# Causal masks of two attentions: from a matmul into the scores to an addition on VectorE

## The reference

```python
# part 1: latent self-attention, 16 heads; q and k have 128 plain and 64 rotated columns
scores = jnp.einsum('bqhd,bkhd->bhqk', q, k) * scale
causal = jnp.tril(jnp.ones((seq_len, seq_len), dtype=bool))
scores = jnp.where(causal[None, None], scores, -jnp.inf)
probs = jax.nn.softmax(scores.astype(jnp.float32), axis=-1)
out = jnp.einsum('bhqk,bkhd->bqhd', probs, v)

# part 2: cross-attention to 375 context rows, 16 heads of 32 columns
scores = jnp.einsum('bhqd,bhkd->bhqk', qh, kh) * inv_sqrt_d
causal = jnp.tril(jnp.ones((sq, sk), dtype=bool))      # row i sees context rows 0..i
scores = jnp.where(causal, scores, jnp.finfo(scores.dtype).min)
attn = jax.nn.softmax(scores, axis=-1)

# part 3: a shared feed-forward network and a mixture of 16 experts, two of them for each row
```

## Time and profile before

| | |
|---|---|
| median of three runs | 857.99 us (857.32 to 858.27) |
| the profiled execution | 858.94 us |
| its span, from first to last instruction | 857.1 us |
| TensorE busy | 827.0 us, 96% |
| VectorE busy | 518.0 us, 60% |
| ScalarE busy | 470.3 us, 55% |
| Pool busy | 241.7 us, 28% |
| granted TensorE clock, mean | 0.996 |

### The profile page before, as it was taken

One profiled execution on the slowest core, in us unless ns is written; L12 is line 12 of the kernel. 1 busy time (PEld: TensorE's weight loads), 2 busy tenths in 40 slices (PEclk: granted clock), 3 DMA queues, 4 the chain that ended last, 5 costly groups with the idle time before them and its releaser, 6 DMA issues.

```text
span 857.1 us, 13364 instructions
## 1 busy us (share of the span) xinstructions
PE 827.0 (96%) x4302; PEld 706.4 (82%) x4302; DVE 518.0 (60%) x962; ACT 470.3 (55%) x1221; POOL 241.7 (28%) x284
## 2 busy tenths in 40 slices
PE   7999999999999999999998899999999999999997
PEld 5887887888788777888877689888888988889885
DVE  4755654753664548687787566355665655646466
ACT  6427545753843556977785526063755737647050
POOL 0142320230132031655654002602233322321420
PEclk9999999999999999999999999999999999999999
DMA  9113225315132406322120113624563655644422
GB/s 336 67 44 111 74 53 152 121 43 160 73 96 51 153 23 213 87 59 57 50 70 24 53 47 85 259 85 150 174 218 117 229 172 184 199 140 144 130 79 86
DMA packets 41597, 99.99 MB, mean 117 GB/s; under 512 B 15888, under 2 KB 23952, under 8 KB 39920
## 3 DMA queue, kind: packets, MB, share of 16 engines
q1 hardware_dynamic: 30496, 61.62, 23.0%
q0 software_dynamic: 11056, 37.79, 13.6%
HBM read 71.59 MB, written 20.97 MB: 108 GB/s over the span
## 4 chain that ended last, share of the span: by engine, by line
PE 77%; issue 9%; ACT 4%; DVE 4%; SPq 2%; DMA 2%; POOL 1%; POOLq 0%; ACTq 0%; DVEq 0%
PE ps L1545 61%; PE ps L1894 2%; PE ps L1566 2%; PE ps L1778 2%; SPq L556 2%; PE ps L1605 2%; PE ps L1884 1%; ACT Pt L885 1%; PE ps L1709 1%; PE ps L1597 1%; DMA stage<-in_wa 1%; PE ps L1896 1%; PE ps L1632 1%; PE ps L1560 1%; PE ps L1718 1%
## 5 line engine op out<-in xcount | busy, mean ns | idle before, releaser
L642 POOL TENSOR_TENSOR Pt<-Pt,rowinv 112x448 f32<-112x448 f32 x64 | 59.7, 933 | 188.2 <-DVE rowinv L1155 187.8
L1545 PE MATMUL ps<-x2T_hi,ws_hi 128*128 128x448 f32 x256 | 95.8, 374 | 3.7 <-ACT h_hi L1020 3.7
L885 ACT ACTIVATE Pt<-ps,negmax 112x112 f32<-112x112 f32 x256 | 87.1, 359 | 19.3 <-DVE negmax L1148 19.1
L1545 PE MATMUL ps<-x2T_hi,ws_lo 128*128 128x448 f32 x256 | 94.3, 368 | 0.0
L1545 PE MATMUL ps<-x2T_lo,ws_hi 128*128 128x448 f32 x256 | 94.2, 368 | 0.0
L1019 ACT ACTIVATE hf<-ps,b 128x448 f32<-128x448 f32 x64 | 40.5, 633 | 93.0 <-PE ps L1545 73.9
L1545 PE MATMUL ps<-w_hi,h_hi 128*128 128x512 f32 x224 | 89.9, 401 | 0.0
L1545 PE MATMUL ps<-w_hi,h_lo 128*128 128x512 f32 x224 | 88.4, 395 | 0.0
L1545 PE MATMUL ps<-w_lo,h_hi 128*128 128x512 f32 x224 | 88.4, 395 | 0.0
L1092 DVE TENSOR_TENSOR h_lo<-hf,h_hi 128x448 fp32r<-128x448 f32 x64 | 39.8, 623 | 47.0 <-ACT h_hi L1020 46.6
L1431 DVE TENSOR_TENSOR acc<-ps,acc 128x512 f32<-128x512 f32 x56 | 38.6, 689 | 45.0 <-PE ps L1545 38.1
(11 more groups left out here) (291 smaller groups left out, 2225.8 us busy)
## 6 DMA issues: line engine op xcount, KB each, us to landing
stage<-in_wf SPq DMA_DIRECT2D x30, 513.0 KB
rows_in<-in_zeros SPq DMA_DIRECT2D x30, 256.0 KB, 4.1
xs<-rows_in POOLq DMA_DIRECT2D x29, 256.0 KB, 4.3
rows_out<-yb POOLq DMA_DIRECT2D x29, 256.0 KB
stage<-in_wa SPq DMA_DIRECT2D x4, 1408.0 KB, 6.6
stage<-in_wb SPq DMA_DIRECT2D x4, 1280.0 KB, 5.6
qr<-ro_hi SPq DMA_DIRECT2D x64, 56.0 KB, 1.9
qr<-ro_lo SPq DMA_DIRECT2D x64, 56.0 KB, 1.9
```

Source lines behind the costliest of these rows:

```text
L642: nc.gpsimd.tensor_tensor(p, p, rowinv[0:S, b % 2, :].unsqueeze(2).broadcast_to([S, GH, S]), ALU.mult).then_inc(norm_done, 1)
L885: last = nc.scalar.activation(Pt[0:S, b % 2, h * S:(h + 1) * S], ps[0:S, b % 2, h * S:(h + 1) * S], ACT.Exp, bias=negmax[0:S, b % 2, h:h + 1],
L1545: ins = mm(dst, w, x, start=start and i == 0, stop=stop and i == len(ops) - 1, skip_group_check=not (start and stop))
```

## The change

The 64 mask matmuls go, with `identb`, `maskb`, their casts and the semaphore for them. Two float32 masks stay in SBUF instead: `maskf` for scores with keys on partitions, `maskq` for scores with queries on partitions; one more transfer brings the second. In self-attention, the turned scores now leave their bank on VectorE, which adds `maskf` on the way to `sT`, at the places ("G", j) of its order; ScalarE's copy goes. In the last group VectorE's list gets a place for G7. In cross-attention, the one reduction of a batch becomes `masked_max`: a memset of a small tile, and for each head an instruction that adds `maskq` to the scores in their PSUM bank, multiplies by -1, writes the result back in place, and takes the minimum of each row, which is the negated maximum. The exponentials take the scores with a scale of -1. Pool gets one more wait, in the loop, ahead of its share of splitting the cross weights (`wx_hi`). The diff, without the places where only a count of a semaphore changes:

```diff
-    ("Z", 3), ("T", 4), ("S", 5), ("N", 5), ("Z", 4), ...
+    ("Z", 3), ("T", 4), ("S", 5), ("G", 7), ("N", 5), ("Z", 4), ...
...
-        identb = sb("identb", [P, S], BF16, at=both)
-        maskb = sb("maskb", [P, S], BF16, at=both)
+        maskf = sb("maskf", [P, S], at=both)
+        maskq = sb("maskq", [P, S], at=both)
+        touch = sb("touch", [P, 2], at=both)
...
-            for dst, name in ((ident, "ident"), (maskf, "mask"), (wnorm, "wnorm")):
+            for dst, name in ((ident, "ident"), (maskf, "mask"), (maskq, "maskq"), (wnorm, "wnorm")):
...
+                else:
+                    pool.wait_ge(x_free["V"], XJ.count(("V", 1), g - 1))
                 high(wx_hi[:, cols], stage[:, cols]).then_inc(xk_hi, 1)
...
-            copy(identb[0:S, :], ident[0:S, 0:S])
-            copy(maskb[0:S, :], maskf[0:S, :]).then_inc(const_done, 1)
...
-            def probabilities(m, b):
+            def probabilities(m, b, sign=1.0):
...
-                                                bias=negmax[0:S, b % 2, h:h + 1],
+                                                bias=negmax[0:S, b % 2, h:h + 1], scale=sign,
...
-                elif kind == "G":
-                    act.wait_ge(job_done, at.number + 1)
-                    copy(sT[0:S, j % 2, :], ps[0:S, 6 + at.bank, 0:GH * S]).then_inc(a_free["G"], 1)
...
+            def masked_max(m, b):
+
+                dve.wait_ge(sc_done, m + 1)
+                nc.vector.memset(touch[0:S, b % 2:b % 2 + 1], 0.0)
+                for h in range(GH):
+                    s = ps[0:S, b % 2, h * S:(h + 1) * S]
+                    ins = nc.vector.tensor_tensor_reduce(s, s, maskq[0:S, :], -1.0, 3.0e38, ALU.add, ALU.min,
+                                                         negmax[0:S, b % 2, h:h + 1])
+                ins.then_inc(max_done, 1)
...
+                elif kind == "G":
+                    dve.wait_ge(job_done, at.number + 1)
+                    nc.vector.tensor_tensor(sT[0:S, j % 2, :].rearrange("p (h s) -> p h s", h=GH),
+                                            ps[0:S, 6 + at.bank, 0:GH * S].rearrange("p (h s) -> p h s", h=GH),
+                                            maskf[0:S, :].unsqueeze(1).broadcast_to([S, GH, S]), ALU.add)\
+                        .then_inc(a_free["G"], 1)
...
-                    row_max(m + j, j)
+                    masked_max(m + j, j)
...
-                    mask(bank[0:S, 0:GH * S], maskb, identb)
...
-                        ins = mm(heads(bank[0:S, 0:GH * S]), w, x, start=False, stop=i == len(ops) - 1,
-                                 skip_group_check=True)
+                        ins = mm(heads(bank[0:S, 0:GH * S]), w, x, start=i == 0, stop=i == len(ops) - 1)
...
-                    mask(ps[0:S, j % 2, 0:GH * S], identb, maskb)
...
-                        ins = mm(ps[0:S, j % 2, 0:GH * S], w, x, start=False, stop=i == 2,
-                                 skip_group_check=True)
+                        ins = mm(ps[0:S, j % 2, 0:GH * S], w, x, start=i == 0, stop=i == 2)
```

More of the change, by code:

```diff
@@ L368, in build @@
         krt = sb("krt", [P, 2, HALF], at=first)
-        maskf = sb("maskf", [P, S], at=first)
         first.close()
@@ L475, in build @@
         yg_ld = [sem(f"yg_ld{i}") for i in range(4)]
-        (const_done, in_hi, in_lo, down_done, sq_done, root_done, rinv_done, nat_done,
+        (in_hi, in_lo, down_done, sq_done, root_done, rinv_done, nat_done,
          kvn_hi, kvn_lo, tr_done, tr_hi, tr_lo, kr_done, kr_mul, kr_rot, krh, krl) = map(sem, (
-            "const_done in_hi in_lo down_done sq_done root_done rinv_done nat_done kvn_hi "
+            "in_hi in_lo down_done sq_done root_done rinv_done nat_done kvn_hi "
             "kvn_lo tr_done tr_hi tr_lo kr_done kr_mul kr_rot krh krl").split())
@@ L830, in _ @@
             copy(wd_hi[:, :, D:768], wd[:, :, D:768]).then_inc(in_hi, 1)
-            act.wait_ge(c_ld, 64)
-            copy(identb[0:S, :], ident[0:S, 0:S])
-            copy(maskb[0:S, :], maskf[0:S, :]).then_inc(const_done, 1)
+            act.wait_ge(c_ld, 80)
             def squares(r):
@@ L978, in x_step @@
                 elif kind == "S":
-                    probabilities(m + j, j)
+                    probabilities(m + j, j, -1.0)
                 elif kind == "T":
@@ L1108, in _ @@
             low(wd_lo[:, :, D:768], wd[:, :, D:768], wd_hi[:, :, D:768]).then_inc(in_lo, 1)
-            dve.wait_ge(c_ld, 64)
+            dve.wait_ge(c_ld, 80)
             def rms(r):
@@ L1593, in heads @@
                 return ap.rearrange("p (h s) -> p h s", h=GH)
-            def mask(dst, w, x):
-                mm(heads(dst), w[0:S, :], x[0:S, :].unsqueeze(1).broadcast_to([S, GH, S]), start=True,
-                   stop=False, skip_group_check=True)
             def transposes(m, b):
@@ L1638, in keys_ready @@
                 pe.wait_ge(krl, 2)
-                pe.wait_ge(const_done, 1)
             def att_step(item, g, at):
@@ L1986, in layouts @@
     o["ident"] = np.eye(P, dtype=f)
-    o["mask"] = np.where(np.arange(P)[:, None] < np.arange(S), f(-3.0e38), f(0))
+    o["maskq"] = np.where(np.arange(P)[:, None] < np.arange(S), f(-3.0e38), f(0))
+    o["mask"] = np.where(np.arange(P)[:, None] > np.arange(S), f(-3.0e38), f(0))
     part = np.arange(P)
```

## The result

The changed kernel takes **870.57 us** (median; 870.25 to 872.62) against 857.65 of the kernel before on the same chip: ratio 1.0156, 95% interval 1.0138 to 1.0173. The forecast was 869, so the time came out as forecast, and slower as forecast. That the sum came out so close is in part luck: self-attention cost more than its term and cross-attention less, and two effects that were in no term, a lower clock and the place of the buffers, have opposite signs.

What follows compares the result with a forecast made beforehand. TensorE was taken to bound the kernel, but VectorE's queue to delay it in self-attention and VectorE to become the bound in cross-attention. 858.94 + 4.3 + 6.8 = 870.0, less 0.95: 869 us; range 858.5 to 880.

Steps and rivals of the forecast that it cites:

- Part 1: TensorE's mask matmuls: 64 go, 0.19 us of queue each, 12.2 us in all if nothing else moves.
- walk over the cross groups: Cross-attention loop group, order lists followed: +1.5 us at c = 1.25, 0 at 1.0, about -0.9 at 0.81.
- c: Cross-attention's masked maximum on VectorE: time from one batch's first to the next instruction, 1.25 us, +0.72 a batch.
- Part 2: Self-attention's turned scores leaving on VectorE, 32 times: late in its in-order queue, +4.3 us, bounds +3.5 to +5.5.
- the first step: Self-attention group: G1's way out stands behind SB1's low half on VectorE, so G2 starts 1.47 us later.
- The second step: End of a self-attention loop group: G5's way out comes only after N3 on VectorE, so E0 starts 1.71 us later.
- E0: TensorE's item of the next self-attention group that uses G5's bank, not a run; forecast start 162.81 instead of 161.10.
- Part 3: Cross-attention's maximum, 32 times: one reduction becomes a memset and four masked instructions on VectorE, +6.8 us.
- Part 4: Small changes: one more mask transfer, two casts gone, a new wait on Pool; 0, at worst +0.5 us.
- Slow heads: Rival, cross-attention's maximum: each instruction waits until the one before has drained, c 1.6 to 2.0, 879 to 887 us; chance 0.19.
- Cheap heads: Rival, cross-attention: c 0.8 to 1.0, TensorE keeps the bound there, 859.8 to 863.3 us; chance 0.19.
- TensorE bound everywhere: Rival, whole kernel: late places made good, c under 1, saved mask matmuls count, 846 to 855 us; chance 0.08.

Runs made afterwards that it cites:

- The part alone: Against the kernel before: under Part 2, only the self-attention change, 865.93 us, ratio 1.0087; under Part 3, only the cross-attention change, 861.31 us, ratio 1.0036.
- the wide filling: The changed kernel with 9 matmuls of no use, 448 wide, on TensorE ahead of G2 and the next group's E0: 867.94 us, ratio 1.0120.

## Why the prediction was right, and where its steps were not

- **Part 1, 0.19 us for a mask on TensorE: the price stands, the paying out did not.** The kernel without the cross mask shows 0.19 (1.00 less 0.81). The forecast never booked 12.2, but its walk over the cross groups counted 26.7 of TensorE's work as a floor that would be reached at small c. Left out, the cross masks give 1.8 us of 6.1, those of self-attention 2.5 of 6.1.
- **Part 2, the queue place: right in place, the first step right in size.** SB1's low half stands ahead (1.93 forecast, 1.92 measured); turned around, the loss goes. The second step is larger than forecast: from SB1's low half to E0 it is 17.7 in a group with the clock up between them (222.48 to 240.19), where the forecast had 17.27 and the kernel before 15.56. SA0's low half, which takes 1.27 in place of 0.96 there, is 0.3 of that; why is open. What failed is the sentence that TensorE carries the delay on unchanged: behind the longer waits it also runs at the lower clock. That step is missing from the sum; it is 3.0 to 5.4 us of the changed kernel's loss. The part alone measures +7.7 against +4.3; less its two stretches at 1.2 to 1.5 us it is +4.7 to +5.3, inside the bounds of 3.5 to 5.5. By the wide filling, which has no stretch, it is +3.9 and, without the place in SBUF, +5.7, just above them.
- **Part 3, c: mis-sized.** 0.91 instead of 1.25, because the accumulator's read runs beside the next head. ScalarE's pair of instructions was the nearest row and the wrong analogue. The 0.15 a head in the upper end had no row either; the read shows 0.14, and overlaps.
- **Part 3, what c does to the group: mis-sized the other way.** At 0.91 the walk gives about -0.7; the part alone gives +3.1, and +4.6 without the place in SBUF (5.2 in the traces). VectorE did not become the bound by its sum (24.26 of 29.60 busy, where the forecast looked for over 26); single chains lengthened: the values' low half behind two maxima, then the way out of the output. How much each of them takes is shown for the first alone. The walk, made by busy time and the share of idle time that stays, took slack for granted that no row had shown. The forecast +6.8 came near +4.6 only since the two errors have opposite signs.
- **Part 4: right**; nothing in the start of the trace after is later than before.
- **The place in SBUF, -1.4 to -1.9: not foreseen,** and not to be seen in any row of the kernel before.
- **Why 869 was hit all the same.** The clock (3.0 to 5.4 too little), the place (1.4 to 1.9 too much) and cross-attention's masked maxima (some 2 too much) were all left out or mis-sized, and they nearly cancel. That is luck; the sign and the first waits are not.
- **Rivals.** Slow heads: out, by the 0.23 a head. Cheap heads had c right (0.8 to 1.0) and the time wrong, as it rested on the same walk. TensorE bound everywhere: out twice, for self-attention by the waits, for cross-attention by the kernel without its mask, which gains only 1.8 even with no new work on VectorE.
- **The sum of the parts:** 7.7 + 3.1 = 10.8, and the changed kernel has 12.9 to 14.0; the intervals of the three are together some 2.5 us wide to each side. The number of stretches of lower clock may be the rest, as the changed kernel has more of them than the part alone in one of two traces; that is argued, not shown.

## What to carry to other kernels

Moving work from a full engine to an idle one is decided by the place in the receiving engine's queue, not by its busy share: here the same instructions cost 12 to 14 us more at one place than at another. Before counting on a saved instruction of the fullest engine, leave it out and measure; an engine that is busy to 99.9% can have chains of nearly the same length beside it. And a sum that comes out right is no proof of its terms: run the parts alone.

## What the runs showed of the hardware that was not expected

- TensorE's granted clock fell to its lower level for some 3.5 us behind waits of 1.9 to 2.4 us (spacing of 448-wide matmuls 0.37 instead of 0.20), behind four of seven in one trace of the changed kernel and two of seven in the other, and behind none in the one trace where matmuls of no use, 448 wide, filled the wait. With 64-wide ones two stretches were left. One stretch cost 1.2 to 1.6 us.
- VectorE's add, minimum and accumulator of 112x112 from and into PSUM takes 305 ns and lets the next in after 0.23; the accumulator's read, 140 ns, overlaps with the next head; a memset of one column beside it (0.06) shows no cost.
- 456 bytes more in front of the buffers made 512-wide matmuls of self-attention nearly 2% faster (some 230 against 234 ns from start to start) and self-attention 1.9 us shorter.
